# Four-layer graph and attention kernel: a head's rows of q and k brought in six transfers in place of eight

## What is computed

```python
h = relu(layernorm(x));  x = x + (adj @ h) @ W0 + b0
h = relu(layernorm(x));  x = x + norm_adj @ (h @ W1) + b1
h = relu(layernorm(x));  x = x + L2(h, adj)   # 8 heads of 32, masked where adj == 0, then proj, ln
h = relu(layernorm(x));  x = x + L3(h, adj)   # 8 heads of 32, scores + (1 - adj) * -1e9, then Wo
```

```python
q, k, v = split into 8 heads of 32
attn = softmax(mask(q @ k.T / sqrt(32)));  o = attn @ v
```

## Time and profile before

| | |
|---|---|
| median of 3 runs | 2760.8 us |
| the profiled execution | 2763.15 us |
| its span (first to last instruction) | 2761.3 us |
| mean granted TensorE clock | 0.994 of full speed |
| PE busy | 2683.8 us, 97% of the span |
| VectorE busy | 2240.1 us, 81% |
| ScalarE busy | 2020.7 us, 73% |
| POOL busy | 1384.1 us, 50% |
| head loads (L753) | 1024 DMAs, 128.0 KB each |

### The profile page before, as it was taken

The page is one execution under the profiler, slowest core; times in us unless marked ns, Lnnn a source line. Parts: engine busy times, 40 slices in busy tenths (PEclk is TensorE's granted clock), DMA queues, the critical chain, the costliest instruction groups (busy, mean ns, idle before and its releaser), DMA issues.

```text
span 2761.3 us, 59344 instructions
## 1 busy us (share of the span) xinstructions
PE 2683.8 (97%) x22552; PEld 2111.9 (76%) x22552; DVE 2240.1 (81%) x4047; ACT 2020.7 (73%) x3678; POOL 1384.1 (50%) x1600
## 2 busy tenths in 40 slices
PE   8999999899999999999999989999999999999999
PEld 7888888677777777777777767777777777777776
DVE  6867676778888888888888878888787888888877
ACT  3000001788888888888888878888888888888887
POOL 2222221246767676767676758453535353536343
PEclk9999999999999999999999999999999999999999
DMA  3001001656666666565656675656566666666655
GB/s 134 31 31 62 30 32 42 176 151 162 159 163 161 162 160 161 150 168 149 170 148 174 158 215 148 180 138 175 141 169 153 161 159 159 156 158 159 157 147 138
DMA packets 438090, 389.70 MB, mean 141 GB/s; under 512 B 43680, under 2 KB 394128, under 8 KB 437808
## 3 DMA queue, kind: packets, MB, share of 16 engines
q1 hardware_dynamic: 420480, 365.04, 50.7%
q0 software_dynamic: 17328, 20.87, 2.9%
HBM read 140.12 MB, written 94.89 MB: 85 GB/s over the span
## 4 chain that ended last, share of the span: by engine, by line
PE 64%; POOL 7%; DMA 3%; SPq 3%; issue 2%; DVE 2%; ACT 2%; DVEq 0%; POOLq 0%; ACTq 0%
PE t_ring_ps L976 23%; PE t_ot_ps L1013 14%; PE t_s_ps L961 14%; PE t_ring_ps L944 4%; PE t_ring_ps L946 4%; PE t_ring_ps L945 4%; POOL t_oT_raw L1655 3%; DMA turned_rows<-t_turned_T 2%; DMA t_R_ot<-inverse_row_sums 1%; SPq L796 1%; POOL t_ot L1637 1%; PE t_ring_ps L1045 1%; POOL t_xe L1573 1%; ACT t_T L1226 1%; DVE t_T L1323 1%
## 5 line engine op out<-in xcount | busy, mean ns | idle before, releaser
L1323 DVE CUSTOM_DVE_ANT_0 t_T<-t_s_ps,mask 128x1024 f32<-128x1024 f32 x1024 | 1226.7, 1212 | 85.0 <-PE t_s_ps L961 79.7
L1226 ACT ACTIVATE t_T<-t_T,t_low 128x1024 f32<-128x1024 f32 x1024 | 1174.0, 1153 | 68.2 <-DVE t_low L1323 66.4
L976 PE MATMUL t_ring_ps<-ident,t_T 128*128 128x128 f32 x7168 | 965.3, 275 | 22.2 <-DVE t_xe L1402 12.4
L976 PEld LDWEIGHTS t_ring_ps<-ident,t_T 128*128 128x128 f32 x7168 | 826.1, 141 | 192.4 <-issue 61.7
L1234 ACT ACTIVATE PT<-t_ring_ps 128x512 f32<-128x512 f32 x1344 | 750.2, 597 | 220.6 <-PE t_ring_ps L976 213.5
L961 PE MATMUL t_s_ps<-t_k,t_q 128*128 128x512 f32 x2048 | 731.0, 438 | 4.4 <-DVE t_low L1323 4.3
L1013 PE MATMUL t_ot_ps<-PT,shared 128*32 128x256 f32 x8192 | 496.8, 383 | 9.8 <-DMA PT<-turned_rows 9.8
L1013 PEld LDWEIGHTS t_ot_ps<-PT,shared 128*32 128x32 f32 x8192 | 240.9, 110 | 234.7 <-issue 58.7
L1422 DVE COPY PT<-t_ring_ps 128x512 f32<-128x512 f32 x448 | 308.0, 688 | 100.2 <-PE t_ring_ps L976 96.4
L961 PEld LDWEIGHTS t_s_ps<-t_k,t_q 128*128 128x128 f32 x2048 | 310.1, 191 | 47.8 <-DVE t_low L1323 35.5
L273 ACT ACTIVATE g_yT_hi<-g_ps 128x512 fp32r<-128x512 f32 x64 | 38.3, 598 | 379.3 <-PE g_ps L205 379.3
(11 more groups left out here) (178 smaller groups left out, 3869.0 us busy)
## 6 DMA issues: line engine op xcount, KB each, us to landing
turned_rows<-t_turned_T SPq DMA_DIRECT2D x128, 512.0 KB, 3.4
PT<-turned_rows SPq DMA_DIRECT2D x512, 128.0 KB, 2.7
t_q<-t_st_hi SPq DMA_DIRECT2D x256, 128.0 KB, 2.3
t_q<-t_st_lo SPq DMA_DIRECT2D x256, 128.0 KB, 2.4
t_k<-t_st_hi SPq DMA_DIRECT2D x256, 128.0 KB, 2.4
t_k<-t_st_lo SPq DMA_DIRECT2D x256, 128.0 KB, 2.6
t_R_ot<-inverse_row_sums SPq DMA_DIRECT2D x252, 64.0 KB, 2.2
t_oT_raw<-t_ot POOLq DMA_DIRECT2D x504, 32.0 KB, 2.8
```

What stands on the lines that cost most here:

```text
L976: last = nc.tensor.transpose(banks[b][:, i * P:(i + 1) * P], T[u % RING][:, kt * P:(kt + 1) * P], ident[:])
L1226: nc.scalar.activation(T[u % RING][:], T[u % RING][:], ACT.Exp, bias=low[:, u % RING:u % RING + 1], scale=-1.0, accum_out=rsum[:, u:u + 1] ...
L1323: nc.vector.tensor_tensor_reduce(out=T[u % RING][:], in0=s_ps[u % 2][:], in1=mask[:, qt, :], scale=1.0, scalar=3.4e38, op0=ALU.add, op1=AL ...
```

## The change

`st_hi` for q and k become the two halves of one buffer `staged_hi`, `st_lo` those of `staged_lo`, and `q4[s]`, `k4[s]` those of `qk4[s]`. Part 0 of a head is the high part for both q and k, and part 3 is the low part for both: each of these goes in one DMA of 32 rows of 8192 bytes. Parts 1 and 2 take the high part of one and the low part of the other and stay four DMAs of 4096-byte rows. The two waits for the splits of q and of k now both stand ahead of the first DMA of the head. The counts on `head_in` go from 128 to 96 for a head.

```diff
-        st_hi = [sb(f"st_hi{i}", [P, N], F32R) for i in range(2)]
-        st_lo = [sb(f"st_lo{i}", [P, N], F32R) for i in range(2)]
-
-        q4 = [sb(f"q4_{i}", [P, N], F32R) for i in range(2)]
-        k4 = [sb(f"k4_{i}", [P, N], F32R) for i in range(2)]
+        staged_hi, staged_lo = sb("st_hi", [P, 2, N], F32R), sb("st_lo", [P, 2, N], F32R)
+        st_hi, st_lo = ([part[:, w, :] for w in range(2)] for part in (staged_hi, staged_lo))
+
+        qk4 = [sb(f"qk4_{i}", [P, 2, N], F32R) for i in range(2)]
+        q4, k4 = ([qk4[i][:, w, :] for i in range(2)] for w in range(2))
...
-                for w, to in enumerate((q4, k4)):
+                for w in range(2):
                     if staged == "first":
 
                         b, n = place["first", FIRST.index(("qk", 0, w, 1))]
...
                         sp.wait_ge(part_split, split_count(staged[0], ("qk", staged[1], w, 1)))
-                    for part in range(4):
-                        dst = slice(part * HD, (part + 1) * HD)
-                        half = (st_hi, st_lo)[part % 2 if w else part // 2]
-                        sp.dma_start(to[s][dst, :].bitcast(F32), half[w][rows, :].bitcast(F32)).then_inc(head_in[s], 16)
+                for part, half in ((0, staged_hi), (3, staged_lo)):
+                    sp.dma_start(qk4[s][part * HD:(part + 1) * HD].bitcast(F32), half[rows].bitcast(F32)).then_inc(head_in[s], 16)
+                for part, halves in ((1, (st_hi, st_lo)), (2, (st_lo, st_hi))):
+                    for w in range(2):
+                        sp.dma_start(qk4[s][part * HD:(part + 1) * HD, w, :].bitcast(F32),
+                                     halves[w][w][rows, :].bitcast(F32)).then_inc(head_in[s], 16)
...
-                    pe.wait_ge(head_in[h % 2], 128 * (4 * job + h // 2 + 1))
+                    pe.wait_ge(head_in[h % 2], 96 * (4 * job + h // 2 + 1))
...
-                        act.wait_ge(head_in[s], 128 * (4 * job + 2 * g))
+                        act.wait_ge(head_in[s], 96 * (4 * job + 2 * g))
...
-                        dve.wait_ge(head_in[s], 128 * (4 * job + 2 * g))
+                        dve.wait_ge(head_in[s], 96 * (4 * job + 2 * g))
```

## The result

The changed kernel takes 2805.8 us (median of 4 runs, 2802.5 to 2811.0) against 2760.2 us before (4 runs, 2759.3 to 2762.3). The ratio is 1.0165, with a 95% interval of 1.0151 to 1.0179: **45.6 us slower**. The prediction was 2773.3 us with a range to 2784: the sign was right, the size was a quarter of what came.

The account below looks back on a forecast made before the run. PE was taken to bound the kernel, with 64% of the chain. Boundaries 8.5, start 2.0 and middle of job 7 2.2, less 0.2, gave +12.5 us: 2773.3 us against 2760.8, range 2761 to 2784.

Parts of the forecast that it names:

- The tight boundary that was worked through: After job 5: head 7's placing stalls PE 1.5 us, overlapping the delay of head 0's chain; +1.5 us together.
- The middle of job 7: Head 4's load behind large weight loads: PE's 3.49 us wait for the turned tile grows by 2.2 us.
- Eleven are usual at 0 to 0.5, 3 us together.: Eleven of 15 job boundaries have reserves that leave only 0 to 0.5 us each, 3 us together.
- change of layer: Boundary after job 7, counted among the four tight ones at 1.0 to 2.1 us.
- The four called tight: Boundaries after jobs 2, 5, 7 and 12, at 1.0 to 2.1 us each, some 5.5 us together.
- Six take 3.8 us.: A head load's six issues on SP take 0.63 us each, leaving the DMA engines 0.9 us of work.
- 2.2 leaves 0.2 of a stall: After job 13: head 7's placing, 2.2 us later, lands just past PE's need and stalls it 0.2 us.
- The idle time of 1.48 leaves 2.2 − 0.3 − 1.48 = 0.4: After job 13: SP's idle time ahead of head 0's move absorbs most of the delay, leaving 0.4 us.
- Start of job 0: 512 KB more after k's split delays the turned tile; PE's 2.86 us wait grows by 2.0 us.
- Engines not the limit: Rival: a merged transfer moves 256 KB in the time of one; +2.0 us, 2763 us; chance 0.22.
- The issue grows with the bytes: Rival: a merged issue takes 1.2 us, so SP is 2.5 us late behind k's split; 2785 us; chance 0.13.
- SP's queue is the limit: Rival: shorter loads gain 1.27 us at three places, boundaries absorb the moved wait; 2757 us; chance 0.08.

Follow-up runs that it names:

- The two runs on it: Changed kernel with only head 0 of job 8 loaded as before: 1.0144; first loads as before with only that one as changed: 1.0008.
- a shorter queue alone: Changed kernel with heads 0 and 4 loaded in eight transfers and the old wait order, six transfers for the other heads: 2761.2 us, ratio 0.9998.
- The swap: Row sums read ahead of the placing of head 0 at job boundaries: 2744.0 us on the kernel before, 2775.5 us on the changed kernel.

## Why the prediction was right and wrong

Right were the sign, the place and the way. The loss comes from the moved wait and not from the transfers' number, and it enters at the turned tile behind the load of head 0. It reaches PE by the two ways that were named, the placing of head 7 and the chain of head 0: at the boundaries 24.1 us more of waits stand at the first and 6.0 at the second. The size was wrong: 45.6 us where 12.5 were forecast. That the bytes and not the issues are the limit held too: with all bytes the load of head 1 has the engines 0.93 busy at 222 GB/s,

```profile
1343.90:1348.40 4.50, 3.63 (x47) 2.47 (x45) 3.98 (x7) 4.50 (x10) 0.00 (x0) 1.00 0.93 222
```

against 0.94 and 208 before. The tight boundary that was worked through came out near its forecast in the sum, 1.6 us after job 5 against 1.5. Its parts did not: the stall at the placing was 0.86 us in place of 1.5, and the other 0.7 came at POOL's split result, so the agreement is partly luck. The middle of job 7 waits 5.19 in place of 3.49 us for its placing: 1.7 against 2.2.

*Fell: "Eleven are usual at 0 to 0.5, 3 us together."* This is the step that failed most. In PE's two waits all 15 boundaries measured 30.1 us: 24.1 at the placings, 9.0 of them at the change of layer, and 31.0 − 25.0 = 6.0 at POOL's split result. The four called tight (2, 5, 7, 12) make 11 of these against 5.5; the eleven usual ones make 19 against 3. Three readings behind it were wrong.

- *"Six take 3.8 us."* An issue was priced by its own row, 0.63 us. Behind full engines it took longer: after job 5 six take 4.6 us in the load of head 1 (before, eight took 5.0) and 5.6 in that of head 0, where POOL's transfers share the engines. The line views, duration of an issue in ns (min/median/max), after:

```profile
L751 SPq DMA_DIRECT2D t_qk<-t_st_hi x128: 512/513/1566, 480.9 to 2752.8; - x128
L751 SPq DMA_DIRECT2D t_qk<-t_st_lo x128: 512/592/2009, 481.5 to 2753.3; - x128
```

```profile
L754 SPq DMA_DIRECT2D t_qk<-t_st_hi x256: 576/642/2121, 482.1 to 2756.7; - x128
L754 SPq DMA_DIRECT2D t_qk<-t_st_lo x256: 507/882/2698, 482.9 to 2755.9; - x128
```

  So the move is issued 3.0 us late instead of 1.27 (medians of the table above), and lands 2.5 late, near the 2.2 that was taken.
- *"2.2 leaves 0.2 of a stall"* (after job 13). The delay was carried to the placing's landing unchanged. It grew on the way. The placing began 2.4 us later, and its last transfer landed after 3.7 us in place of 2.8, since the load of head 1 comes right behind it. The line view of L798 at that placing:

```profile
  PE t_ot_ps L1015: 1.6, 1
...
DMA to landing us min/median/max: 2.2/2.6/3.7
```

  PE was ready at the same 13.85 us after k's split in both kernels, so a reserve of 1.9 us (the time by which the placing had landed ahead of PE's need) became a stall of 1.6.
- *"The idle time of 1.48 leaves 2.2 − 0.3 − 1.48 = 0.4"* (after job 13). SP's idle time was taken as slack of the whole path. SP's part did shrink like that: there the move of head 0 is issued only 0.4 us later. But the idle time had let the load of head 1 land: its last transfer landed 0.4 us after the move's issue before, and 2.6 us after it now. So the tile takes 4.15 us in place of 3.20 and lands 1.4 us later (0.5 and 1.7 in the medians over the boundaries). Had the working asked both for SP and for the engines, as it did for head 7, it would have found this.

*Left out: the granted clock.* Nothing in the sum allowed that PE would run slower. PE's busy time grew by 11.9 us, the largest term that the sum lacked. Rows of before could have told: half-clock stretches already stood at some of these boundaries (PE busy 3.29 us of 3.30 at PEclk 0.54 behind the 1.91 us wait after job 5). A forecast that lengthens such waits has to price what may follow them. How the 43.0 us divide between waits and clock is read from busy and idle time; no run changes the clock alone.

```profile
1352.70:1356.00 3.30, 3.29 (x16) 3.29 (x17) 0.46 (x1) 0.00 (x0) 2.85 (x3) 0.54 1.17 315
```

(That window is of the kernel before.)

*The change of layer* was one of the four tight boundaries at up to 2.1 us. In the trace its two waits of PE grew by 9.01 − 3.95 = 5.1 us. The two runs on it give 2.8 and 5.8, within noise of each other and of the forecast. That the long transfer comes from the mask loads is read from the timelines; moving those was not tried.

*Start of job 0*, forecast +2.0 at the placing, with q and k late by as much, "which nobody notices". PE waits 3.07 us for q and k there, which it did not before, and then less for the placing (1.58 for 2.86). That makes 1.8 us, near the 2.0 but by another way, so the match is luck. It does not last: before, `values` of head 0 ran at the lower clock behind the 2.86 us wait (506.5 to 509.9), with the change they do not, and at head 1 the delay is 0.3 us. *The other loads of head 4*, forecast to add nothing: three do, 1.2 us together, in jobs 2, 3 and 8.

By the sum's terms: boundaries 30.1 for 8.5, middle of job 7 1.7 for 2.2, start 1.8 for 2.0, clock 11.9 for nothing, other middles 1.2 for nothing. That is 46.7 against the 43.0 of the two spans; the rest lies in waits that shrank.

**The rivals.** *Engines not the limit*, where a merged transfer passes as quickly as a single one, is out by the 45.6 us, the share of 0.93 and the kernels with half the bytes. *The issue grows with the bytes* came nearest in time (2785), but its row is wrong: the merged issues take 0.51 and 0.59 us. It is the ones behind that grow. In effect it described SP's delay behind k's split better than the forecast did: 2.5 us against 3.0 measured, where the forecast had 1.27. That the load of head 1 gives nothing back is nearly so (0.4 us after job 5). *SP's queue is the limit* is out: a shorter queue alone gave 0.9998.

## What to carry to other kernels

Here the transfers that were issued while the queue would have waited anyway cost nothing. Merging them with ones whose data comes later moved their bytes into the busy time, and what stood behind them in that queue was late. So before two waits are joined, count the bytes that stand ahead of the later one, not the issues that are saved. Slack has to be read twice, once in the issuing queue and once on the DMA engines, and a stall of PE is priced with what its clock may do after it (some 1.6 us here, six times in 14).

## What the runs showed of the hardware that was not expected

- An issue on SP of the same 4096-byte rows takes 0.5 to 0.6 us while the engines have room, and a median of 0.88, at most 2.70 us, for one part of the load behind two merged transfers. The issue time followed the bytes: with half of them six issues take 3.8 us, with all 5.6.
- The load of head 1 moved 222 GB/s at a share of 0.93 in merged transfers and 213 at 0.88 in single ones (medians over jobs 1 to 15, worked out from the traces, with whatever else ran beside them). No run's time shows that difference.
- Lengthening PE's waits at 13 boundaries by 0.8 us each (20.4 to 30.3 us in all, without the change of layer), beside new waits for placings, went with six stretches at 1.2 GHz, worth some 1.6 us each. The swap that shortened those waits went with less time at the lower level, 30.7 us in place of 58.0.
- A 512 KB transfer took 14.95 us when eight mask loads from POOL started right behind it, and 4.5 us when it was issued 3.0 us ahead of them.
